# Two transposes moved off TensorE in a four-layer graph network: x3 through a DRAM scratch, the adjacency in blocks

## The reference

```python
x = _layernorm(x + gat(x, adj))        # layer 0: attention, 4 heads ("pre")
x = _layernorm(x + gru(x, adj))        # layer 1: 3 GRU steps over neighbours ("gru")
x = _layernorm(x + relational(x, adj)) # layer 2: sum_r (adj == r) @ x @ W_r + bias ("rel"), r = 1..4
x = _layernorm(x + gat(x, adj))        # layer 3: attention, 1 head ("post")

def gat(h, adj):                       # per head
    Wh = h @ W
    e = leaky_relu((Wh @ a1)[:, :, None] + (Wh @ a2)[:, None, :], 0.2)
    return elu(softmax(where(adj > 0, e, NEG_INF)) @ Wh)
```

## Time and profile before

| | |
|---|---|
| time, median of 3 runs | 2617.78 us (2617.44 to 2618.26) |
| profiled execution: span from first to last instruction | 2616.2 us |
| TensorE (PE) busy | 2564.6 us (98%) |
| VectorE (DVE) busy | 2064.6 us (79%) |
| ScalarE (ACT) busy | 1629.9 us (62%) |
| GpSimd (POOL) busy | 1093.8 us (42%) |
| mean granted TensorE clock | 0.992 |

### The profile page before, as it was taken

One profiled execution on the slowest core, in us unless ns is written; L12 is line 12 of the kernel. 1 busy time (PEld: TensorE's weight loads), 2 busy tenths in 40 slices (PEclk: granted clock), 3 DMA queues, 4 the chain that ended last, 5 costly groups with the idle time before them and its releaser, 6 DMA issues.

```text
span 2616.2 us, 48544 instructions
## 1 busy us (share of the span) xinstructions
PE 2564.6 (98%) x14979; PEld 2219.6 (85%) x14979; DVE 2064.6 (79%) x5210; ACT 1629.9 (62%) x4153; POOL 1093.8 (42%) x1264
## 2 busy tenths in 40 slices
PE   7999999999999999999999999999999999999995
PEld 6888888888888888888888888888888888888884
DVE  7877887877887877887877887877887877887765
ACT  5556665666665666665666665666665666665553
POOL 1333444443444443444443444443444443444342
PEclk9999999999999999999999999999999999999997
DMA  5212121112121212111212121212121212121000
GB/s 166 78 39 54 33 52 46 52 50 58 32 53 44 54 50 58 32 53 43 54 50 58 31 54 42 55 50 58 31 54 42 55 49 58 31 55 38 27 13 21
DMA packets 265105, 128.99 MB, mean 49 GB/s; under 512 B 139760, under 2 KB 249840, under 8 KB 264816
## 3 DMA queue, kind: packets, MB, share of 16 engines
q1 hardware_dynamic: 245120, 107.97, 15.8%
q10 hardware_dynamic: 19696, 17.44, 2.0%
HBM read 108.27 MB, written 17.08 MB: 48 GB/s over the span
## 4 chain that ended last, share of the span: by engine, by line
PE 94%; DVE 1%; issue 1%; ACT 0%; POOL 0%; POOLq 0%; DVEq 0%; ACTq 0%
PE psum L938 60%; PE psum L792 10%; PE psum L926 6%; PE psum L853 6%; PE psum L975 3%; PE psum L842 3%; PE psum L869 2%; PE psum L811 1%; PE psum L913 1%; PE psum L861 1%; DVE stats L1351 0%; ACT x L1176 0%; POOL rstd L1508 0%; DVE first_scores L1322 0%; DVE moments L1355 0%
## 5 line engine op out<-in xcount | busy, mean ns | idle before, releaser
L938 PE MATMUL psum<-ag_h,wc_h 128*128 128x512 f32 (+1 forms) x1188 | 489.0, 412 | 2.7 <-issue 2.0
L938 PE MATMUL psum<-ht_h,whh_h 128*128 128x512 f32 (+1 forms) x1188 | 483.0, 407 | 0.7 <-ACT g_z L1159 0.6
L938 PE MATMUL psum<-ht_h,whh_l 128*128 128x512 f32 (+1 forms) x1188 | 462.8, 390 | 0.0
L938 PE MATMUL psum<-ag_l,wc_h 128*128 128x512 f32 (+1 forms) x1188 | 461.9, 389 | 0.0
L938 PE MATMUL psum<-ht_l,whh_h 128*128 128x512 f32 (+1 forms) x1188 | 461.7, 389 | 0.0
L938 PE MATMUL psum<-ag_h,wc_l 128*128 128x512 f32 (+1 forms) x1188 | 461.5, 388 | 0.0
L1506 POOL TENSOR_SCALAR rstd<-moments 128x2 f32<-128x2 f32 x256 | 73.3, 286 | 858.6 <-DVE moments L1355 854.1
L1557 POOL TENSOR_TENSOR ht<-ht,g_n 128x512 f32<-128x512 f32 (+1 forms) x198 | 251.7, 1271 | 71.3 <-ACT g_n L1164 63.7
L938 PEld LDWEIGHTS psum<-ht_h,whh_l 128*128 128x128 f32 x1188 | 224.9, 189 | 50.8
L938 PEld LDWEIGHTS psum<-ag_h,wc_l 128*128 128x128 f32 x1188 | 223.4, 188 | 50.5
L938 PEld LDWEIGHTS psum<-ht_l,whh_h 128*128 128x128 f32 x1188 | 225.7, 190 | 40.0
(11 more groups left out here) (152 smaller groups left out, 6218.3 us busy)
## 6 DMA issues: line engine op xcount, KB each, us to landing
first_scores<-first_kept SPq DMA_DIRECT2D x116, 256.0 KB, 3.7
adj_i<-in_adj_dram SPq DMA_DIRECT2D x128, 128.0 KB, 3.2
x_in<-in_x_dram SPq DMA_DIRECT2D x64, 256.0 KB, 3.8
out_dram<-out_t ACTq DMA_DIRECT2D x64, 256.0 KB, 2.5
x_blocks<-in_x_dram SPq DMA_DIRECT2D x464, 32.0 KB, 2.1
part<-in_adj_dram SPq DMA_DIRECT2D x32, 256.0 KB, 3.3
adj_g<-in_adj_dram SPq DMA_DIRECT2D x31, 256.0 KB, 3.3
last_scores<-last_kept SPq DMA_DIRECT2D x59, 128.0 KB, 3.0
```

The source lines that it names most:

```text
L938: last = mm(dst, s, m, start=(first and k == 0), stop=(last_part and k == len(flat) - 1))
```

## The change

Two turns leave TensorE.

1. x3 of units 0 to 58: SP stores x3 to one of two DRAM scratch tensors (`x3_keep`), waits for the store to land, and loads it back in 32x32 blocks with four DMAs of 64 KB (`x3_blocks`) into the ring of two buffers that `x_blocks` uses; VectorE turns the blocks. The units 59 to 63 stay as they were.
2. The adjacency of layer 2: `post_load` additionally loads it in blocks (four DMAs of 32 KB into one buffer `adj_b`, int32), VectorE turns it into `adj_t` (now int32), and the cast on GpSimd, the TensorE turn and the ScalarE copy are gone.

The blocks of the pre attention come in four DMAs of 64 KB instead of eight of 32 KB. In the table, `att_xt(post,..)` is moved to a later place for both units of a half, and the `att_wh` of the second one is moved behind the two `gru_turn` steps.

```diff
 def blocked(kind, u):

-    return kind == "pre" and u >= BLOCKED
+    return u >= BLOCKED if kind == "pre" else u < POST_BLOCKED


 def takes(step):
@@ -86,13 +86,13 @@
 gru_z(-1,1,1)  att_exp(post,-3,1)
 gru_in(-1,1,1)
 gru_agg(0,0,0)
-gru_agg(0,0,1)  att_spread(pre,1,0,0)  att_spread(pre,1,0,1)  att_store(post,-3,0)  rel_norm(-2,0)  att_res(post,-3,1)
-        att_scores(pre,1,0,0)  att_scores(pre,1,0,1)  pre_load(1,1)
+gru_agg(0,0,1)  att_spread(pre,1,0,0)  att_spread(pre,1,0,1)  att_store(post,-3,0)  rel_norm(-2,0)  x3_keep(-2,0)  att_res(post,-3,1)
+        att_scores(pre,1,0,0)  att_scores(pre,1,0,1)  pre_load(1,1)  x3_blocks(-2,0)
 gru_hn(0,0,0)
-gru_rzh(0,0,0)  gru_n(-1,1,1)  att_xt(post,-2,0)
+gru_rzh(0,0,0)  gru_n(-1,1,1)
 gru_r(0,0,0)  att_prob(pre,1,0)  rel_adjt(-2,1)
 gru_z(0,0,0)
-gru_in(0,0,0)
+gru_in(0,0,0)  att_xt(post,-2,0)
 gru_hn(0,0,1)  att_pt(pre,1,0,0)  att_wh(post,-2,0,0)  gru_new(-1,1,1)  gru_split(-1,1)  att_pt(pre,1,0,1)
         att_wh(post,-2,0,1)  att_rows(post,-2,0)  att_spread(post,-2,0,0)  att_xt(pre,1,1)  rel_mask(-2,1)  gru_n(0,0,0)
 gru_rzh(0,0,1)  gru_turn(-1,1,0)  att_pv(pre,1,0)  gru_new(0,0,0)  att_wh(pre,1,1,0)  att_wh(pre,1,1,1)  att_rows(pre,1,1)
@@ -101,15 +101,16 @@
 gru_z(0,0,1)  rel_rest(-2,1)
 gru_in(0,0,1)
 gru_agg(-1,2,0)  att_prob(post,-2,0)  att_res(pre,1,0)  att_store(post,-3,1)  gru_n(0,0,1)  rel_norm(-2,1)
+        x3_keep(-2,1)
 gru_agg(-1,2,1)
-gru_hn(-1,2,0)  att_pt(post,-2,0,0)
-gru_rzh(-1,2,0)  att_xt(post,-2,1)  gru_new(0,0,1)  gru_split(0,0)  att_pv(post,-2,0)  att_spread(pre,1,1,1)
+gru_hn(-1,2,0)  att_pt(post,-2,0,0)  x3_blocks(-2,1)
+gru_rzh(-1,2,0)  gru_new(0,0,1)  gru_split(0,0)  att_pv(post,-2,0)  att_spread(pre,1,1,1)
         att_scores(pre,1,1,0)  att_scores(pre,1,1,1)
 gru_r(-1,2,0)
-gru_z(-1,2,0)  att_wh(post,-2,1,0)  att_wh(post,-2,1,1)  att_exp(post,-2,0)  att_prob(pre,1,1)  x_blocks(2,0)  pre_load(2,0)
+gru_z(-1,2,0)  att_exp(post,-2,0)  att_prob(pre,1,1)  att_xt(post,-2,1)  x_blocks(2,0)  pre_load(2,0)
         gru_n(-1,2,0)
 gru_in(-1,2,0)
-gru_hn(-1,2,1)  gru_turn(0,0,0)  gru_turn(0,0,1)  gru_load(1)
+gru_hn(-1,2,1)  gru_turn(0,0,0)  gru_turn(0,0,1)  gru_load(1)  att_wh(post,-2,1,0)  att_wh(post,-2,1,1)
...
+POST_BLOCKED = 59
...
+            def post_load(u):
+                load_adj("post_load", u)
+                take(sp, "adjb", "post_load", u)
+                blocks = adj[2 * u:2 * u + 2].rearrange("g (b i) (f j) -> f i (g b) j", i=TURN, j=TURN)
+                for f in range(P // TURN):
+                    sp.dma_start(adj_b[f * TURN:(f + 1) * TURN].rearrange("i (m j) -> i m j", j=TURN), blocks[f]).then_inc(s_adjb, 16)
+
             def pre_load(u):
                 load_adj("pre_load", u)
                 i = take(sp, "x", "pre_load", u)
                 sp.dma_start(x_in[i][:], x[2 * u:2 * u + 2].rearrange("g n d -> n g d")).then_inc(s_x[i], 16)

+            def load_blocks(i, blocks):
+                for f in range(P // TURN):
+                    sp.dma_start(xs[i][f * TURN:(f + 1) * TURN].rearrange("i c (m j) -> i c m j", j=TURN),
+                                 blocks[f].rearrange("i c g b j -> i c (g b) j")).then_inc(s_xs[i], 16)
+
+            def x3_keep(u):
+                sp.wait_ge(s_x3, u + 1)
+                after(sp, LAY["post"].xt_high, u - 1)
+                sp.dma_start(x3_kept[u % 2].rearrange("g n d -> n g d"), x3[slot("x3", "rel_norm", u)][:]).then_inc(s_x3_kept, 16)
+
+            def x3_blocks(u):
+                i = take(sp, "xs", "x3_blocks", u)
+                sp.wait_ge(s_x3_kept, 16 * (u + 1))
+                load_blocks(i, x3_kept[u % 2].rearrange("g (b i) (c f j) -> f i c g b j", i=TURN, f=P // TURN, j=TURN))
+
             def x_blocks(u):
                 i = take(sp, "xs", "x_blocks", u)
-                blocks = x[2 * u:2 * u + 2].rearrange("g (b i) (c f j) -> c f i g b j", i=TURN, f=P // TURN, j=TURN)
-                for c in range(C):
-                    for g in range(P // TURN):
-                        sp.dma_start(xs[i][g * TURN:(g + 1) * TURN, c, :], blocks[c, g].rearrange("i g b j -> i (g b) j")).then_inc(s_xs[i], 16)
+                blocks = x[2 * u:2 * u + 2].rearrange("g (b i) (c f j) -> f i c g b j", i=TURN, f=P // TURN, j=TURN)
+                load_blocks(i, blocks)

             def gru_load(k):
                 take(sp, "adjg", "gru_load", k)
@@ -723,7 +748,7 @@
                 sp.dma_start(L.scores[ti][:, 0:n, :].rearrange("p h n -> p (h n)"), kept.broadcast_to([P, n * P])).then_inc(L.spread[q], 16)

...
-            def rel_adjt(u):
-                i = take(pe, "light", "rel_adjt", u)
-                pe.wait_ge(s_adjf, u + 1)
-                for q in range(2):
-                    last = turn(LIGHT[:, i, q * P:(q + 1) * P], adj_f[:, q, :], ident[:])
-                last.then_inc(s_adjt_ps, 1)
...
-            def rel_adjt(u):
-                i = slot("light", "rel_adjt", u)
-                ai = take(act, "adjt", "rel_adjt", u)
-                act.wait_ge(s_adjt_ps, u + 1)
-                f(adj_t[ai][:], LIGHT[:, i, 0:2 * P], ACT.Copy).then_inc(s_adjt, 1)
...
+            def rel_adjt(u):
+                ai = take(dve, "adjt", "rel_adjt", u)
+                dve.wait_ge(s_adjb, 64 * (u + 1))
+                nc.vector.transpose(adj_t[ai][:], adj_b[:]).then_inc(s_adjt, 1)
...
-                    stand(pool)
-                    nc.gpsimd.tensor_copy(adj_f[:], adj_i[i][:]).then_inc(s_adjf, 1)
...
```

More of the change, by code:

```diff
@@ L289, in placed @@
     u = 2 * k - 1 + a[1]
-    if name == "x_blocks" and not blocked("pre", u):
+    if name == "x_blocks" and not blocked("pre", u) or name in ("x3_keep", "x3_blocks") and not blocked("post", u):
         return []
@@ L384, in bass_gnn_stack @@
         ht = [None, sb("ht1", [P, C, 4 * P])]
-        adj_t = [sb(f"adj_t{i}", [P, 2 * P]) for i in range(SLOTS["adjt"])]
+        adj_t = [sb(f"adj_t{i}", [P, 2 * P], I32) for i in range(SLOTS["adjt"])]
         hr_t = sb("hr_t", [P, C, 2 * P])
@@ L405, in bass_gnn_stack @@
         x2_b = sb("x2_b", [P, 2, D])
-        adj_f = sb("adj_f", [P, 2, P])
+        adj_b = sb("adj_b", [P, 2 * P], I32)
         mt1, mtr = sb("mt1", [P, 2, P]), sb("mtr", [P, 2, P])
@@ L418, in bass_gnn_stack @@
         Y_OF = {"pre": 0, "post": 1}
+        x3_kept = [nc.dram_tensor(f"x3_kept{i}", (2, P, D), F32, kind="Internal").ap() for i in range(2)]
         class Layer:
@@ L567, in bass_gnn_stack @@
         ROWED = {kind: [s[2] for s in order if s[:2] == ("att_rows", kind)] for kind in ("pre", "post")}
+        TURNED = [s[1:] for s in order if s[0] == "att_xt" and blocked(*s[1:])]
         DIRECT = {kind: [s[2:] for s in order if s[:2] == ("att_direct", kind)] for kind in ("pre", "post")}
@@ L609, in last_read @@
                 }[resource, name]
-            if name == "x_blocks":
-                return s_xturned, a[0] - BLOCKED + 1
+            if name in ("x_blocks", "x3_blocks"):
+                return s_xturned, TURNED.index(("pre" if name == "x_blocks" else "post", a[0])) + 1
             if name == "pre_load":
@@ L615, in last_read @@
             if name == "post_load":
-                return {"adj": (LAY["post"].pen_ready, a[0] + 1), "adjf": (s_adjt_ps, a[0] + 1),
+                return {"adj": (LAY["post"].pen_ready, a[0] + 1), "adjb": (s_adjt, a[0] + 1),
                         "post_pen": (LAY["post"].masked, a[0] + 1)}[resource]
@@ L1051, in att_xt @@
                 if blocked(kind, u):
-                    act.wait_ge(s_xturned, u - BLOCKED + 1)
+                    act.wait_ge(s_xturned, TURNED.index((kind, u)) + 1)
                     src = xt_f[:].rearrange("p c n -> p (c n)")
                 else:
-                    act.wait_ge(L.xt_psum, u + 1)
+                    act.wait_ge(L.xt_psum, u + 1 if kind == "pre" else u - POST_BLOCKED + 1)
                     src = LIGHT[:, slot("light", "att_xt", kind, u), :]
@@ L1289, in att_xt @@
                 if blocked(kind, u):
-                    i, rounds = ring("xs", "x_blocks", u)
-                    dve.wait_ge(s_xs[i], 128 * (rounds + 1))
+                    i, rounds = ring("xs", "x_blocks" if kind == "pre" else "x3_blocks", u)
+                    dve.wait_ge(s_xs[i], 64 * (rounds + 1))
                     nc.vector.transpose(xt_f[:], xs[i][:]).then_inc(s_xturned, 1)
@@ L1494, in load @@
                 pool.wait_ge(s_adj[i], 16 * (rounds + 1))
-                if kind == "post":
-                    take(pool, "adjf", "post_load", u)
-                    stand(pool)
-                    nc.gpsimd.tensor_copy(adj_f[:], adj_i[i][:]).then_inc(s_adjf, 1)
                 pi = take(pool, kind + "_pen", kind + "_load", u)
```

27 lines of the change are left out of this document (14 added, 13 removed).

## The result

| | before | after |
|---|---|---|
| median (range) | 2618.02 us (2617.44 to 2622.21) | 2911.43 us (2909.54 to 2913.53) |
| ratio, 95% interval | | 1.112 (1.1104 to 1.1135) |
| span of the profiled execution | 2616.2 us | 2911.6 us |
| mean granted clock over the span | 0.992 | 0.947 |

The change costs 293 us; 208 were forecast. The page of the changed kernel: span, busy time, and the costliest group that waits.

What follows compares the result with a forecast made beforehand. TensorE, busy throughout the steady state, was taken as the bound: 2616.2 us of span - 39 for removed turns + 191 and 56 for waits = 2824, so 2826 us as median was predicted, range 2700 to 2920.

Steps and rivals of the forecast that it cites:

- the sum: Whole kernel: 2616.2 us of span less 39 for removed turns plus 191 and 56 of waits gives 2824 us.
- The bound: Steady state: TensorE alone, busy 800 of 800 us, sets the time; work removed is gained and waits lost one to one.
- The removed turns: TensorE: 364 turns of x3 and adjacency leave, at 0.108 us each, for -39 us.
- The even unit: Second unit of a half: TensorE waits 6.6 us for `xt_l` ahead of `att_wh`, 29 times, +191 us.
- The odd unit: First unit of a half: TensorE waits 1.9 us for `xt_l` ahead of `att_wh`, 29 times, +56 us.
- whatever makes TensorE wait is a loss one to one: Steady state: each wait of TensorE costs its own length, with the granted clock at its upper level of 2.4 GHz.
- spread not late: Second scores of the pre unit: their spread is on time, even wait only 2.9 us, 2718 us; chance 0.13.
- the 9.2 of the bound: Even unit with a timely spread: VectorE gains 2.04 plus 0.69 us, so masks end at 1205.60, x3 complete at 1196.39.
- The gain comes through: TensorE: the removed turns give 39 us and no wait appears, 2579 us; chance 0.13.
- Slow blocks: Small blocks read from the scratch are slow: waits of 9.7 and 4.4 us, up to 2988 us; chance 0.07.

Runs made afterwards that it cites:

- the filler: Changed kernel plus 27 useless 512-column products ahead of TensorE's wait in the even units 2 to 56; 2848.74 us.
- early-spread kernel: Changed kernel with the second spread of the pre scores issued by SP ahead of the store of x3; 2833.95 us.
- The best order that was found: Changed kernel with that spread issued ahead of x3's store and every `att_wh` moved behind later gate products (even post one behind `gru_z`); 2614.87 us, ratio 0.9989.
- the adjacency alone: Only the adjacency part of the change: x3 turned on TensorE and the step table as in the kernel before; 2604.04 us.

## Why the prediction was right, and by how much it was off

- **The outcome.** Slower, as forecast, but by 293 us instead of 208. The range ends at 2920, 9 us above the result, and its upper side stood for slow transfers, which the runs exclude; that it also covers a term that the sum did not have is luck.
- **The bound.** Right: TensorE alone sets the time, and no wait of it is given back. That a wait costs just its own length was wrong, see "What the sum lacked".
- **The removed turns, -39 us.** 0.108 us each was nearly right: the adjacency gave 12.8 us of span for 14, x3's turns 0.4 us a unit for 0.43. Together 36. (A turn of the adjacency on VectorE took 0.44 us, where 0.35 was assumed; it is in no chain.)
- **The even unit, 6.6 us, 191.** Measured 6.7 us, 29 times: 194. The steps and their order were right. That the total is only 0.1 us off is luck, since the sizes of single steps were off and cancelled: the store 2.2 us for 2.5, four block issues 2.6 for 1.94 (fewer DMAs of twice the size are not issued at the old rate), the spread 3.9 for 3.7, the gates and exponential up to the first of the eight 1.7 for 1.97. The Trainium skill's page "DMA: Bandwidth & Descriptors" (Anatomy of one DMA) gives its fit for DMAs that GpSimd issues. The estimate from it, 2.6 us for store and spread alike, is met by neither of these DMAs of SyncE: 2.2 and 3.9 us.
- **The odd unit, 1.9 us, 56.** Measured 1.65 us: 48. VectorE's queue was a little earlier than counted.
- **What the sum lacked.** With measured values it is 2616 - 36 + 194 + 48 = 2822 us, and the span is 2911.6. The failing step is "whatever makes TensorE wait is a loss one to one": a wait of 6.7 us cost 9.1 to 9.5. The clock falls during it, and the next 5.6 us of work run at half pace. By rows that is 81 us; the filler, in 28 of the 29 halves, gave back 63 to 70. The whole trace closes the sum: TensorE's idle time is 248 us more than before (290.6 against 42.8; the two waits are 242 of it), the lower clock costs 80, and what remains is -32 for the removed turns, 4 short of the 36. The earlier trace rows showed 1.00 throughout, but a kernel without waits can't show what a wait does to the clock; that was no reason to leave the term out.
- **The rival "spread not late", 2.9 us.** It was too kind: the wait is 4.8. The bound said VectorE would gain the 2.04 us that it waited for ScalarE and 0.69 us of work. In the early-spread kernel it waited 1.57 us for GpSimd's `ht` at the same place instead: masks end 11.3 us after x3 is complete, 11.9 in the earlier trace rows (1208.33 less 1196.39), and not the 9.2 of the bound.
- **"The gain comes through".** No kernel here did that. The best order that was found reached 2614.9 us, 11 more than the adjacency alone. The 23 us of x3's turns are paid for by 21 us more of idle time (66.9 against 45.7), mostly the 0.4 and 0.3 us of new waits a half, and by restarts: around the wait for `first_turned` the starts of the products lie 0.24 us further apart than the wait explains, around that for `mt` 0.12 to 0.19, together some 11 us. Whether an order exists in which they come through was not settled.
- **"Slow blocks".** Excluded: x3's blocks issue and land like those of x (2.4 and 2.5 us on the page of the changed kernel).

## What to carry to other kernels

When one engine is full, a unit of work taken from it is worth its pace in the stream (here 0.1 us a turn), and each chain that grows longer for it must be followed to the moment at which that engine arrives; if it arrives first, price the wait and then the work behind it at the lower clock. Before a chain's latency is attacked, move the waiting instruction: with the changed data path as it was, placing four steps elsewhere, with what hangs on them, gave back 297 us. A DMA that waits delays all that is queued behind it on its issuing engine, so look there first for who else is late.
